# Router stage of a graph-attention and expert kernel: unread wide products on TensorE, constants on GpSimd

## The reference

```
x = x + relu(attention(layernorm(x), src, dst))          # 4 heads of 64, summed over the edges of a node
xn = layernorm(x); xn2 = layernorm(xn) * gamma + beta
logits = xn2 @ Wr + br                                   # 2500 x 8
top_vals, top_idx = top_k(logits, 2); w = softmax(top_vals)
y = sum over the two chosen e: w_e * (gelu(xn2 @ W1[e] + b1[e]) @ W2[e] + b2[e])
out = x + y
```

## Time and profile before

| | |
|---|---|
| median of 3 runs | 1257.93 us (1257.76 to 1258.65) |
| the profiled execution, its own time | 1254.97 us |
| its span | 1253.2 us |
| PE busy | 660.4 us (53% of the span) |
| DVE busy | 729.4 us (58%) |
| POOL busy | 785.5 us (63%) |
| mean granted clock of PE | 0.759 |
| last product of the attention begins | 949.9 us after the span's start |
| router stage, from there to the first gather of the experts (L539) | to 1013.2 us |

### The profile page before, as it was taken

The page is one execution under the profiler, slowest core; times in us unless marked ns, Lnnn a source line. Parts: engine busy times, 40 slices in busy tenths (PEclk is TensorE's granted clock), DMA queues, the critical chain, the costliest instruction groups (busy, mean ns, idle before and its releaser), DMA issues.

```text
span 1253.2 us, 10981 instructions
## 1 busy us (share of the span) xinstructions
PE 660.4 (53%) x2658; PEld 526.1 (42%) x2658; DVE 729.4 (58%) x1782; ACT 410.8 (33%) x1035; POOL 785.5 (63%) x835
## 2 busy tenths in 40 slices
PE   0530343355435643465435643366447459999990
PEld 0520232244223432244223432244336448888880
DVE  6711476558665676557665686557778843333325
ACT  3550243144322443144422443234521412222210
POOL 5577777777777777777777777777700025555540
PEclk9975667786678766777667776777777569999995
DMA  8464434444444434444344443444490212222217
GB/s 282 171 122 109 109 107 110 109 111 109 107 109 111 109 106 109 109 111 110 106 110 109 111 109 107 110 110 107 137 364 9 84 33 68 72 76 72 68 59 254
DMA packets 79451, 143.95 MB, mean 115 GB/s; under 512 B 22337, under 2 KB 50467, under 8 KB 79267
## 3 DMA queue, kind: packets, MB, share of 16 engines
q0 software_dynamic: 39664, 110.31, 31.7%
q1 hardware_dynamic: 37147, 30.44, 8.0%
q10 hardware_dynamic: 2584, 2.56, 0.6%
HBM read 126.48 MB, written 17.40 MB: 115 GB/s over the span
## 4 chain that ended last, share of the span: by engine, by line
POOL 50%; PE 19%; issue 18%; DVE 6%; DMA 2%; PEld 1%; ACT 1%; PEldq 1%; DVEq 0%; POOLq 0%
POOL ring L528 48%; PE psum L727 8%; PE psum L741 7%; PE psum L591 1%; POOL ring L500 1%; PEld psum L640 1%; PE psum L715 1%; PEldq L642 1%; PE psum L682 1%; DVE acc L1460 1%; DVE acc L1461 1%; PE psum L673 1%; ACT ring L878 1%; DMA ring<-in_dst,ring 1%; DMA h_tab<-ring 0%
## 5 line engine op out<-in xcount | busy, mean ns | idle before, releaser
L528 POOL DMA_INDIRECT ring<-h_tab,srcP x664 | 630.9, 950 | 204.4 <-issue 202.0
L640 PE MATMUL psum<-ring,shared 128*128 128x260 f32 x1328 | 389.2, 450 | 446.5 <-DVE acc L1101 388.4
L640 PEld LDWEIGHTS psum<-ring,shared 128*128 128x128 f32 x1328 | 285.9, 224 | 536.6 <-DVE acc L1101 403.9
L822 ACT ACTIVATE shared<-iota_f,Dcol 128x128 f32<-128x128 f32 x664 | 202.0, 386 | 33.2 <-PEq L642 33.2
L1188 DVE TENSOR_TENSOR ring<-ring,psum 128x2048 f32<-128x2048 f32 x83 | 189.8, 2287 | 2.8
L1101 DVE TENSOR_TENSOR acc<-acc,psum 128x260 f32 x332 | 140.0, 422 | 61.0 <-PEq L642 24.8
L840 ACT ACTIVATE Ex<-Z 128x128 f32<-128x128 f32 x21 | 6.5, 309 | 513.0 <-DVE Z L1155 513.0
L1123 DVE STREAM_TRANSPOSE TB<-ring 128x128 f32<-128x128 f32 x21 | 8.5, 403 | 222.8 <-DMA ring<-h_tab,srcP 222.8
L539 POOL DMA_INDIRECT ring<-z_tab,ring x54 | 52.5, 972 | 117.5 <-DVEq L1399 101.3
L548 POOL DMA_INDIRECT ys_tab<-shared,ring x54 | 54.3, 1005 | 87.6 <-DVE shared L1419 79.3
L727 PE MATMUL psum<-ring 128*128 128x256 f32 x432 | 99.5, 385 | 0.0
(11 more groups left out here) (287 smaller groups left out, 610.5 us busy)
## 6 DMA issues: line engine op xcount, KB each, us to landing
ring<-h_tab,srcP POOLq DMA_INDIRECT x664, 2.8
ring<-in_L_ffn_W SPq DMA_DIRECT2D x16, 512.0 KB, 11.5
h_tab<-ring SPq DMA_DIRECT2D x10, 260.0 KB, 2.5
ring<-in_x SPq DMA_DIRECT2D x1, 2432.0 KB
z_tab<-ring SPq DMA_DIRECT2D x2, 1024.0 KB, 4.4
ring<-ys_tab SPq DMA_DIRECT2D x4, 512.0 KB, 9.0
ring<-ys_tab ACTq DMA_DIRECT2D x4, 512.0 KB, 9.6
out<-acc SPq DMA_DIRECT2D x4, 512.0 KB
```

What stands on the lines that cost most here:

```text
L528: pool.indirect_dma_start(out=ring[:, t % RING, :], out_offset=None, in_=h_tab, in_offset=bass.IndirectOffsetOnAxis(ap=srcP[:, t:t + 1], a ...
L640: pe.matmul(sums[G_at % NSUM][:, 0:MW], dst_oh[:, n % OHB, 2 * g + r, :], ring[:, t % RING, :], start=(r == 0), stop=(r == 1))
L822: last = act.activation(dst_oh[:, n % OHB, k, :], iota_f[:, :], ACT.Square, scale=-1.0, bias=Dcol[:, t:t + 1])
```

## The change

Two things are changed. PE gets products whose result nobody reads: `unread(width)` multiplies `ones` with the first columns of `shared` into PSUM bank 7. Six of 512 columns stand behind the last batch, and one of 256 columns stands between `nodes_T(i + 1)` and `router(i)`, nine in all. They wait for nothing and raise nothing. The constants that DVE made behind its scales are made by GpSimd instead, behind its wait for the last batch, and DVE waits for them ahead of L1314's product.

```diff
+            pool.wait_ge(batch_done, NBAT)
+            pool.memset(upper, 1.0).then_inc(late_ones, 1)
+            pool.memset(valid, 1.0).then_inc(late_ones, 1)
+            pool.memset(carry_on[:, :, 1:NB], 1.0).then_inc(late_consts, 1)
+            pool.memset(carry_on[:, :, 0:1], 0.0).then_inc(late_consts, 1)
+            for into, pattern, base, mult in ((e_less, ...), (gran, ...), (spare, ...), (pair_f, ...)):
+                pool.iota(into, ...).then_inc(late_consts, 1)
+            pool.tensor_copy(iota_b, iota_f[:, :]).then_inc(late_consts, 1)
+            pool.wait_ge(late_ones, 2)
+            for into, pattern, base in ((upper, [[1, P]], -1), (valid, [[-P, NB]], N - 1)):
+                pool.affine_select(out=into, in_=into, compare_op=ALU.is_ge, ...).then_inc(late_consts, 1)
             pool.wait_ge(where_ready, 1)
...
+            def unread(width):
+
+                pe.matmul(bank[7][:, 0:width], ones[:, :], shared[:, 0:width], start=True, stop=True)
+
+            for _ in range(6):
+                unread(512)
             nodes_T(0)
             for i in range(NB // 2):
                 if i + 1 < NB // 2:
                     nodes_T(i + 1)
+                    unread(256)
                 router(i)
...
-            c.link(v.tensor_scalar(upper, iota_f[:, :], pcol[:, 0:1], None, ALU.is_gt))
...      (eleven instructions of DVE, L1294 to L1304)
-            c.link(v.tensor_scalar(pair_f, iota_f[:, 0:PAIRS], 1.0, None, ALU.add))
...
+            v.wait_ge(late_consts, 9)
             v.wait_ge(norm_ready, len(SETS))
```

More of the change, by code:

```diff
@@ L328, in gat_moe_kernel @@
         x_again_in = [sem(f"x_again_in{n}") for n in range(len(SETS))]
+        late_ones, late_consts = sem("late_ones"), sem("late_consts")
         z_stored, table_in, table_done, where_ready = (
@@ L551, in put_slots @@
                         in_=y_out[:, u, m, :], in_offset=None).then_inc(y_put[u], 16)
+            pool.wait_ge(batch_done, NBAT)
[3 more added lines that the diff above has]
+            pool.memset(carry_on[:, :, 0:1], 0.0).then_inc(late_consts, 1)
+            for into, pattern, base, mult in ((e_less, [[1, NE]], -NE, 0), (gran, [[BS, EG]], 0, 0),
+                                              (spare, [[P, NH]], (PAIRS + 1) * P, 1), (pair_f, [[1, PAIRS]], 1, 0)):
+                pool.iota(into, pattern=pattern, base=base, channel_multiplier=mult,
+                          allow_small_or_imprecise_dtypes=True).then_inc(late_consts, 1)
+            pool.tensor_copy(iota_b, iota_f[:, :]).then_inc(late_consts, 1)
+            pool.wait_ge(late_ones, 2)
+            for into, pattern, base in ((upper, [[1, P]], -1), (valid, [[-P, NB]], N - 1)):
+                pool.affine_select(out=into, in_=into, compare_op=ALU.is_ge, fill=0.0, base=base,
+                                   pattern=pattern, channel_multiplier=-1).then_inc(late_consts, 1)
             pool.wait_ge(where_ready, 1)
```

## The result

The changed kernel takes 1263.62 us (median of 5 runs, 1260.99 to 1265.77), the kernel before 1257.76 us (5 runs, 1257.1 to 1258.65). The ratio is 1.0044, 95% interval 1.0032 to 1.0055: 5.9 us slower. The profiled execution took 1260.99 us and is the fastest of the five. In one job of the experiments one of the 31 runs of the kernel before was in a slow state (2284.1 us, the others at most 1395.41) and is left out of the ratios.

The account below looks back on a forecast made before the run. PE at the half clock level was taken to bound the router stage. Eight slow pairs at 0.85 us, less slack, gave 5.2 us, so 1260.2 us profiled; with 2.96 for the median, 1263.1 us, range 1255.3 to 1265.2.

Parts of the forecast that it names:

- The bound: Router stage: PE at the half clock level bounds it at 2.46 us a pair, and DVE has slack.
- The constants: Eleven DVE instructions, about 2.6 us, moved to GpSimd: worth nothing while PE bounds; new wait costs 0.
- The six wide products: 512-column products behind the last batch: about 5.2 us at the full level, covered by PE's wait, cost 0.
- The nine: 256-column products between router pairs: 0.43 us each at full level, 0.85 at half; pairs of 1.74 or 3.31 us.
- The level: PE's clock falls to half between 957 and 963 us and does not rise again in the router stage.
- the wait for the second set: PE's wait of about 2.2 us for DVE's second set of blocks, long enough to lose the full clock level.
- The sum: Router stage: 6.2 us more with all eight pairs slow, 4.7 with one at full level; 5.2 taken.
- DVE's one wait for the logits: DVE's wait for PE before L1317's counterpart, forecast to grow from 1.4 to about 11 us.
- The chance of a return: Rival: the level falls and comes back in the router stage; 0.5 us more after four slow pairs; chance 0.09.
- The likeliest case: The clock level is lost around the second set of blocks and stays at half: 1263.1 us, chance 0.68.
- The half level that the prediction reads in the earlier trace: Eight transposes read as half level, then eight 264-column passes in 2.76 us: leaning against the page that transposes don't count.
- The rival that held the other sign: The level holds through the router stage, ACT becomes the bound: 2.4 us less, 1255.5 us, chance 0.18.

Follow-up runs that it names:

- e1: The changed kernel without any unread product, only the constants moved to GpSimd: ratio 0.9989 to the kernel before, stage time 64.63 us.
- e8: e5 with the constants back on DVE: ratio 0.9978 to the kernel before, stage time 62.01 us.
- e3: Only the six unread products of 512 columns added to the kernel before: ratio 0.9982, stage time 63.78 us.
- e5: The changed kernel with two more unread 512-column products behind pair 0's router products, in PE's wait: ratio 0.9982 to the kernel before, stage time 61.89 us.
- e11: e7 with ACT's Exp moved ahead of its normalise of the last 16 blocks: ratio 0.9965 to the kernel before, stage time 61.64 us.
- e4: Only the nine unread products of 256 columns added to the kernel before: ratio 1.0041, stage time 70.98 us.
- e12: e5 without the six products ahead of the first transposes: ratio 0.9988 to the kernel before, stage time 62.34 us.
- e9: The kernel before with ACT's Exp moved ahead of its normalise of the last 16 blocks: ratio 0.9989, stage time 64.10 us.
- e10: e5 with ACT's Exp moved ahead of its normalise of the last 16 blocks: ratio 0.9956 to the kernel before, stage time 60.04 us.
- e7: e5 without the nine products between the pairs: ratio 0.9975 to the kernel before, stage time 61.95 us.

## Why the prediction was right

*The bound.* PE at the half level bounded the stage: e1 took 2.6 us from DVE and moved nothing.

*The constants.* Forecast 0 on both engines, with DVE waiting 4.0 us for PE. Measured 0.00 us in the stage time and 3.82 us. While the level holds they were forecast to matter a little; e8 shows 0.12 us.

*The six wide products.* Forecast 5.2 us, hidden by the wait, cost 0. Measured 5.41 us with the pipeline's end, wait left 0.29 us, and in e3 no cost but a gain of 0.85.

*The nine.* Forecast 0.43 and 0.85 us each, pairs of 1.74 and 3.31 us. Measured 1.71 us for a pair in e5, and 0.85 and 3.31 us in the chain after. The prices from other lines with the same shapes of weights held to 0.03 us a pair.

*The level.* Forecast to fall between 957 and 963; it fell at 962.3. The cause named, the wait for the second set with thin work ahead, is what e5 tested: two products in that wait, and nothing else changed, turn +5.54 into -2.74 us. The wait isn't the only way to lose it: e11 lost it in thin work with the wait filled. That the level didn't rise again with wide work in each pair is shown by the windows after and by e4.

*The sum.* Between 4.7 us (one pair at the full level) and 6.2 us (none), taken 5.2. The stage time has 5.54: a group of transposes and the first part of one unread product were at the full level, less than a pair. With none, e4 has 6.35. The profiled execution was forecast at 1260.2 us and took 1260.99: 0.34 us more in the stage, 0.87 more ahead of it, and 0.41 less behind it, where the half level lasted 3.4 us into the experts (before 3.9). The median lies 2.63 us above the profiled execution, and 2.96 was assumed. That the total of 1263.62 came within 0.6 us of the forecast is thus in part luck; the stage's share, 5.54 against 5.2, is not. The medians differ by 5.86, and the runs spread over 4.8 us against 1.6 before. A fall one pair earlier or later makes 1.57 us, so it can be a part of that spread and not the whole; the rest is open.

*What was off.* The prediction wanted DVE's one wait for the logits to grow to 11 us. It is two waits, 5.07 us for ACT's last root and 5.53 for PE, 10.6 in all: ACT's root stands behind a copy that waits for PE, which I had used only for the case of a held level. The chance of a return was judged on the earlier trace rows, where some 8 us of dense products went before the rise. e12 doesn't refute that row, for it rose behind 8.2 us without a gap; but it shows that the work need not be wide throughout, as only the last 3.55 us of it was. The likeliest case needed only that a quarter isn't enough, which e4 bears out. The half level that the prediction reads in the earlier trace rows rests on the pace of the products alone: the view's granted clock reads 1.00 in all of that stretch. It is weak evidence on what transposes count for.

*The rival that held the other sign* was priced at -2.4 us, with ACT as the bound; e5, in which the level does hold, has -2.74 (-2.63 at the Exp), and its chain is the one that the rival named.

## What to carry to other kernels

Before adding work that is to keep TensorE's clock up, find each stretch in which the engine will wait or do thin work at the new pace, and price the added work at the half level as well: here the level was lost around an open wait of 2.1 us, the added products made a loss of 5.5 us, and two more in that wait turned it into a gain of 2.7. Filling the waits isn't always enough: without the nine products between the pairs, the level fell there as well (e11). Work of this kind belongs first into the waits, where it costs nothing as long as it is shorter than the wait; inside a chain that bounds it is paid at either level. When a bound is moved, look at once for the next engine: moving one Exp ahead of 8 us of ACT work that nobody waited for gave 1.85 us more, and 0.5 without the rest.

## What the runs showed that I had not expected

The kernel before took about 1256 us in two jobs and 1392 in two others. Nearly all of the difference lies in the attention (first transposes at 956 against 1094 us). The view of waits has this row for GpSimd in e1 (who, for whom, total, times, longest), and none like it in the profile of the kernel before; e9 and e10, of the other slow job, have it too (117.7 and 119.3 us):

```profile
POOL ring L529 <- PEq L658: 116.5, 35, 13.1
```

The gathers waited there for batches to end; what is behind it was not tried. The stage time of e1 is that of the kernel before to 0.01 us all the same.

The level outlasted the last wide product by 7.0 us of transposes and products of 8 columns in e7, and by 3.1 us in e11, with the same program on PE up to there. At the half level the same work did not raise it in the kernel before in 21.6 us without a gap (960.6 to 982.2, PE busy 21.50 us, granted clock 0.50). And the mix of pairs with a product of 256 columns kept the full level in e5 and never regained it in e4.
